# Softmax sums from the exponentials' accumulator, and attention results of two heads in one column group

## What is computed

```
q, k, v  = x @ qkv_weights, split into heads
a        = einsum('aib,ajb->aij', q, k) / 4
a        = tril * a + NEG_INF * (1 - tril)
a        = softmax(a, axis=-1)
heads    = einsum('aij,ajb->aib', a, v)
x        = layernorm(x + heads)
```

## Time and profile before

| | |
|---|---|
| median of 3 runs | 766.68 us (763.91 to 766.88) |
| profiled execution, its time | 762.62 us |
| its span in the profile | 760.7 us |
| mean granted TensorE clock | 0.983 |
| busy over the span: PE, DVE, ACT, POOL | 700.6, 470.8, 449.3, 391.2 us |
| batch stage, first to last exponential | 34.1 to 392.5 us |

### The profile page before, as it was taken

How to read it: one execution, slowest core, us unless ns; L and a number is a source line. 1 busy time by engine, 2 the same in 40 slices (tenths; PEclk the granted TensorE clock), 3 DMA queues, 4 the chain that set the end, 5 groups by cost and what they waited for, 6 DMA issues and landing times.

```text
span 760.7 us, 19153 instructions
## 1 busy us (share of the span) xinstructions
PE 700.6 (92%) x5464; PEld 529.7 (70%) x5465; DVE 470.8 (62%) x1427; ACT 449.3 (59%) x1242; POOL 391.2 (51%) x532
## 2 busy tenths in 40 slices
PE   7968899899999999999997897899999999999983
PEld 6857788788888888888875554555565556565452
DVE  2555578788888889888866554344444444443373
ACT  0268688788888888888863221344444444454154
POOL 1001134235445545544545471477777777777481
PEclk9999999999999999999999999999999999999988
DMA  8744474523223323323455246555555455554883
GB/s 296 260 153 157 134 226 149 191 65 92 72 86 90 81 81 101 110 73 108 113 158 169 80 175 199 146 86 84 84 84 84 84 84 84 84 85 69 250 289 138
DMA packets 84779, 97.98 MB, mean 129 GB/s; under 512 B 12160, under 2 KB 76288, under 8 KB 83680
## 3 DMA queue, kind: packets, MB, share of 16 engines
q1 hardware_dynamic: 59728, 64.03, 27.3%
q0 software_dynamic: 14752, 23.53, 15.6%
q10 hardware_dynamic: 10224, 9.49, 4.7%
HBM read 55.90 MB, written 41.10 MB: 128 GB/s over the span
## 4 chain that ended last, share of the span: by engine, by line
PE 69%; issue 7%; DMA 6%; DVE 6%; POOL 4%; SPq 4%; ACT 2%; ACTq 0%; POOLq 0%; DVEq 0%
PE ps L1034 12%; PE ps L1043 6%; PE ps L797 5%; PE ps L894 4%; PE ps L785 4%; PE ps L762 4%; PE ps L807 4%; PE ps L837 4%; PE ps L897 3%; PE ps L918 3%; PE ps L765 3%; PE ps L817 3%; POOL total L666 3%; DMA attn_only<-in_ctx 2%; PE ps L1020 2%
## 5 line engine op out<-in xcount | busy, mean ns | idle before, releaser
L1109 ACT ACTIVATE prob<-ps,nmax 128x128 f32<-128x128 f32 x512 | 146.9, 379 | 29.8 <-DVE nmax L1308 28.8
L1034 PE MATMUL ps<-first_use,xgT 128*128 x284 | 133.8, 593 | 1.5 <-ACT xgT L1227 1.5
L666 POOL DMA_INDIRECT total<-rot,result_row x71 | 112.1, 1579 | 13.8 <-issue 12.6
L1569 DVE TENSOR_TENSOR tile_parts<-ps,attn_only 128x512 f32<-128x512 f32 x71 | 49.1, 692 | 90.0 <-PE ps L1034 90.0
L1308 DVE TENSOR_REDUCE nmax<-ps 128x4 f32<-128x512 f32 x128 | 82.2, 685 | 21.3 <-PE ps L785 20.2
L599 POOL TENSOR_TENSOR rot<-products 128x128 f32<-128x128 f32 x128 | 61.2, 499 | 65.7 <-DVE products L1318 65.6
L1116 ACT COPY pT<-ps 128x512 f32<-128x512 f32 x128 | 76.9, 601 | 19.2 <-PE ps L797 13.7
L797 PE MATMUL ps<-tf,prob 128*128 128x128 f32 x512 | 78.8, 277 | 6.2 <-ACT pT L1116 6.2
L623 POOL DMA_INDIRECT sent<-packets,pos x64 | 63.4, 991 | 36.9 <-PE ps L785 22.6
L1034 PEld LDWEIGHTS ps<-first_use,xgT 128*128 128x128 f32 x284 | 53.5, 190 | 40.1 <-issue 36.5
L650 POOL TENSOR_TENSOR tile_parts<-tile_parts 128x256 f32<-128x256 f32 x71 | 51.2, 721 | 58.2 <-ACT tile_parts L1222 58.2
(11 more groups left out here) (140 smaller groups left out, 1449.1 us busy)
## 6 DMA issues: line engine op xcount, KB each, us to landing
xg<-sent ACTq DMA_DIRECT2D x68, 130.5 KB, 2.1
first_use<-total SPq DMA_DIRECT2D x12, 512.0 KB, 8.5
total<-zeros POOLq DMA_DIRECT2D x1, 4224.0 KB, 17.8
k_dram<-first_use SPq DMA_DIRECT2D x4, 1024.0 KB, 4.5
attn_only<-in_x_turned SPq DMA_DIRECT2D x32, 128.0 KB, 3.0
attn_only<-k_dram SPq DMA_DIRECT2D x256, 16.0 KB
attn_only<-in_x SPq DMA_DIRECT2D x32, 128.0 KB, 2.7
attn_only<-in_ctx SPq DMA_DIRECT2D x32, 128.0 KB, 2.7
```

The costliest lines, as they stand in the source:

```text
L666: eng.indirect_dma_start(totals[slot % 2], bass.IndirectOffsetOnAxis(ap=result_row[:, slot:slot + 1], axis=0), yw[:, slot % 4, :], None, c ...
L1034: mm = eng.matmul(ps[:, r, :], xgT[:, r, c, :], rw1_sb[:, bass.ds(e * (DC * 2 * FFN) + c * 2 * FFN, 2 * FFN)], start=(c == 0), stop=(c == ...
L1109: ins = eng.activation(prob[:, t % 2, 4 * u + n, :], SCORE[u][:, n * P:(n + 1) * P], ACT.Exp, bias=nmax[:, t % 2, 4 * u + n:4 * u + n + 1])
L1569: eng.tensor_tensor(hid[:, r, :], ps[:, r, :], rb_h[:, bass.ds(e * (2 * FFN), 2 * FFN)], ALU.add).then_inc(hid_set, 1)
```

## The change

Four edits that belong together:

1. Each exponential also gives its row sum to a new tile `den`, by the instruction's accumulating output. `HEAD_OF` says which head stands at which place of which bank.
2. V no longer carries a column of ones. Each head's 32 columns hold 16 of V and 16 zeros: even heads in the first half, odd heads in the second. Two heads write the same 32 rows (one starts the accumulation, the other ends it), so that the 16 heads fill 8 groups of 32 rows, 256 columns of bank 5.
3. The copy to `oT` takes 256 columns in place of 512, and two transposes take the place of four.
4. The reciprocals read `den` and are taken one step earlier, for sequence `n-1`; the multiplication waits for the transposes itself.

```diff
+HEAD_OF = [[2 * u + n % 2 + 8 * (n // 2) for n in range(4)] for u in range(4)]
...
-        HEADS_T = ps[:, 5, :].rearrange("p (x t) -> p x t", t=P)
-        HEADS = ps[:, 5, :].rearrange("p (h v) -> p h v", v=VW)
+        HEADS_T = ps[:, 5, 0:D].rearrange("p (x t) -> p x t", t=P)
+        HEADS = ps[:, 5, 0:D].rearrange("p (h d) -> p h d", d=DH)
...
-        oT = sb("oT", [P, H // CG, P])
+        oT = sb("oT", [P, D // P, P])
+        den = sb("den", [P, 2, H])
...
-            eng.memset(va[:, :, :, DH:DH + 1], 1.0)
...
-                for h in range(H):
-                    lo = h % CG * VW
-                    mm = eng.matmul(HEADS_T[lo:lo + VW, h // CG, :], va[:, t % 3, h, :],
-                                    pT[:, h % 8 // 2, 2 * (h // 8) + h % 2, :], start=True, stop=True)
+                for x in range(D // P):
+                    for e in range(2):
+                        for g in range(CG):
+                            h = 2 * CG * x + 2 * g + e
+                            mm = eng.matmul(HEADS_T[g * VW:(g + 1) * VW, x, :], va[:, t % 3, h, :],
+                                            pT[:, h % 8 // 2, 2 * (h // 8) + h % 2, :], start=(e == 0), stop=(e == 1),
+                                            skip_group_check=True)
...
-                    for b in range(H // CG):
+                    for b in range(D // P):
...
                     ins = eng.activation(prob[:, t % 2, 4 * u + n, :], SCORE[u][:, n * P:(n + 1) * P], ACT.Exp,
-                                         bias=nmax[:, t % 2, 4 * u + n:4 * u + n + 1])
+                                         bias=nmax[:, t % 2, 4 * u + n:4 * u + n + 1],
+                                         accum_out=den[:, t % 2, HEAD_OF[u][n]:HEAD_OF[u][n] + 1])
...
-                    eng.copy(oT[:, :, :].rearrange("p x t -> p (x t)"), ps[:, 5, :]).then_inc(oT_set, 1)
+                    eng.copy(oT[:, :, :].rearrange("p x t -> p (x t)"), ps[:, 5, 0:D]).then_inc(oT_set, 1)
...
-                    eng.copy(va[:, t % 3, :, 0:DH], QV[:, D:2 * D].rearrange("p (h d) -> p h d", d=DH)).then_inc(v_set, 1)
+                    eng.copy(va[:, t % 3, :, :].rearrange("p (j e) (f d) -> p j (e f) d", e=2, d=DH)[:, :, 0:4:3, :],
+                             QV[:, D:2 * D].rearrange("p (j e d) -> p j e d", e=2, d=DH)).then_inc(v_set, 1)
...
-                if live(t2):
-                    eng.wait_ge(heads_turned, t2 + 1)
-                    eng.reciprocal(rden[:, r2, :], HEADS[:, :, DH]).then_inc(den_set, 1)
+                if live(n - 1):
+                    eng.wait_ge(expd, 4 * n)
+                    eng.reciprocal(rden[:, (n - 1) % 2, :], den[:, (n - 1) % 2, :]).then_inc(den_set, 1)
...
                 if live(t2):
+                    eng.wait_ge(heads_turned, t2 + 1)
                     eng.wait_ge(den_set, t2 + 1)
```

More of the change, by code:

```diff
@@ L1469, in step @@
                 if live(t2):
+                    eng.wait_ge(heads_turned, t2 + 1)
                     eng.wait_ge(den_set, t2 + 1)
-                    eng.tensor_tensor(att[:, r2, :].rearrange("p (h d) -> p h d", d=DH), HEADS[:, :, 0:DH],
+                    eng.tensor_tensor(att[:, r2, :].rearrange("p (h d) -> p h d", d=DH), HEADS,
                                       rden[:, r2, :].unsqueeze(2).broadcast_to([P, H, DH]), ALU.mult).then_inc(att_set, 1)
```

## The result

The changed kernel takes 783.74 us (median of 6 runs, 781.11 to 786.45) against 767.32 us before: the ratio is 1.0197, with a 95% interval of 1.0157 to 1.0237. It is slower by 2.0%; the medians differ by 16.4 us. The prediction said 805, which is 38 us more than before, with a range of 774 to 845. The direction and the place were right; the size was not: it forecast more than twice the loss.

What follows compares the result with a forecast made beforehand. PE was taken as the bound, with ACT's ring about 1 us shorter. New step 10.1 + 0.1 + 2.3 = 12.5 us against 11.15, times 28 gives 38 us: 762.6 + 38 = 801, 805 against the median, range 774 to 845.

Steps and rivals of the forecast that it cites:

- The ring from the first exponential over ACT's list to the scaled Q, scores and maximum: Batch-stage cycle through ACT, PE and DVE: 10.1 us without slack against a step of 11.15, to become the longest.
- all holes in ACT's list: ACT's idle gaps between first exponential and scaled Q, 1.0 us per step in all, counted as slack.
- the allowance of 0.1: Per step, for ACT waiting on PE's turn of probability group 2; an allowance, not a measured wait.
- The 28 steps: Of 31 intervals between first exponentials, about 3 are held by something else; 28 x 1.35 = 38 us.
- r = 0.145: Start-to-start cost in us of each accumulator read on ACT; 16 reads add 2.3 us per step.
- my lower end 0.055: Lower bound in us on a read's cost, the fixed part of L1192, an ACT instruction with only immediates.
- the read overlaps but is not free, r about 0.09: Rival on the ACT reads: ring 11.6 us per step, 14 us more, time 780; chance 0.24.
- PE's 0.22: Two of four transposes in L904 go: 0.22 us per step, 7 us over 32 steps, if PE stays the bound.
- PE's ring would be 10.7: PE's own step after the change: about 11.15 - 0.22 - 0.20 = 10.7 us.
- That ends PE's 0.20 us hold before L945: The earlier reciprocal lets DVE's K products start sooner, removing PE's 0.20 us wait per step.
- PE is the longer ring by about 1 us, and no more: In the batch stage, work added to ACT between first exponential and L1192 is paid out of that 1 us.
- The copy of oT, the order of the result matmuls, the memset: Copy 0.22 less on ACT but shortens nothing; paired matmuls cost nothing; dropped prologue memset nothing, 0.18 us if uncovered.

Runs made afterwards that it cites:

- E2: Kernel before the change with only the accumulating sums added to its exponentials, written to a tile nobody reads; ratio 1.0209, median 785.2 us.
- E1: Changed kernel with the accumulating output taken off the exponentials, reciprocals reading ones, result unnormalised; ratio 1.0014 to the kernel before, median 766.9 us.
- E3: Changed kernel with sums on only two of the four exponentials of each bank, other heads unnormalised; ratio 1.0069 to the kernel before, median 771.8 us.
- E6: Changed kernel, all sums, with ACT's copy of group 1 ahead of bank 0's exponentials and x1T's copy behind scaled Q; ratio 1.0137 to before, 770.1 us.

## Why the prediction was wrong

**What bounds the kernel.** Right in its main point. The ring from the first exponential over ACT's list to the scaled Q, scores and maximum became the chain that ends last. It was incomplete: I took all holes in ACT's list for PE's doing, which would vanish when ACT gets later. The hole before the copy of group 2 is a round trip between ACT and PE and stayed whole (0.32 idle in both traces, 0.43 in start-to-start time before and 0.46 after); the allowance of 0.1 for this very wait was too small. And a hole of 0.19 before xv, in the trace of before, I had not seen; 263.63 was possible:

```profile
263.82 0.37 ACT L1159 COPY xv<-ps 128x256 f32<-128x256 f32 x1
```

The two errors, with the 0.1 allowed, nearly cancel, which is luck: 10.1 + 0.1 + 16 x 0.09 = 11.64, against 11.70 measured for that step. The 28 steps are a little many: 28 x 0.58 is 16.2 us, and the batch stage grew by 14.3. The 25 steps outside the start and the arrivals grew by 14.5 and the other six shrank by 0.2.

**The step that failed: r = 0.145.** "I take the exponential's own fixed part" was wrong. The read costs 0.09 start to start, between my lower end 0.055 and the value taken. 16 x 0.055 us too much per step is 0.88 us, and over 28 steps 25 us, which is the distance from 805 to 780; measured were 783.7. This is a term mis-sized and not a mechanism missed, and the rival "the read overlaps but is not free, r about 0.09" named both its price and its time (780), at 0.24. The reads' durations, 0.19 to 0.27, lie near gexp's 0.24, but only the distance of the starts counts. From the Trainium skill's page "ScalarE: Activation LUTs", section "What ACT_TABLE_LOAD costs", I had estimated 94 ns for a one-element instruction with immediates; the trace's 0.09 for the read agrees with that estimate, though the page gives no price for the read itself. The argument that the read "has to deliver a per-partition value" and so costs like a per-partition operand had nothing behind it: what makes the exponential's fixed part longer than that of L1192 may be its operand coming in, and the read has none. That reason I have not tested.

**PE's 0.22.** Right that it is worth nothing beside the late ACT (E2). Wrong that PE's ring would be 10.7 without it: E1 shows 11.22, and 11.02 in its early steps. "That ends PE's 0.20 us hold before L945" failed. The K products do start 0.15 earlier in E1 (1.67 after the first exponential against 1.82), but scx stands behind the Q products, and those wait for PE; the hold is 0.26. "PE is the longer ring by about 1 us, and no more" was too simple as well: in E3 eight reads, 0.73 in all, cost 0.13 to 0.19 per step.

**The copy of oT, the order of the result matmuls, the memset.** Costed at nothing. E1, with all of them in, is 0.11 us per step under before in the early steps and 0.04 over it in the later ones, and its result matmuls hold the chain for 1.01 us as before. So none of them shows a cost, if they do not offset each other.

**The stages behind.** Forecast as untouched. The profiled pair seems to say otherwise; the medians leave some 2 us for them, and the last section deals with the rest.

**What would show it.** 512 reads as a group: yes. Four exponentials in 1.7 us: no, 1.51 from 270.64 to the end of the fourth read. No idle time before x1T: yes. PE idle 1.8 us per step: no, 0.56 in the step from 270.64. Steps of 12.5: no, 11.76. ACT's L1197 as what the scores wait for: yes, as the chain shows.

## What to carry to other kernels

An output that "comes for free" with an instruction can be a second instruction behind it; cost it by start-to-start distances of short neighbours, with both ends, and put the number where it lies between the likeliest rows before choosing by an argument. When an engine is 97% busy, that does not mean that work taken from it shortens the step: look at the events in mid-step that come at a fixed delay from another engine, and ask on which side of them the saved work stands. And a wait between two engines that hand one buffer back and forth is part of the ring and does not vanish when one of them gets slower. Before steps of two profiles are compared at the level of a tenth of a microsecond, look whether the same wait ends at the same delay in both; here a late signal, and not the edit, made up to 0.2 us of such differences.

## What the runs showed of the hardware

**A read of the accumulator** takes 0.19 to 0.27 us and costs 0.09 start to start behind a 128-column exponential. Durations grow along an unbroken run of such pairs, with the starts at even distances: the reads go from 0.19 (270.91) on, the exponentials from 0.36, and the last read of the step reads

```profile
278.99 0.27 ACT L1113 ACTIVATION_READ_ACCUMULATOR prob<-ps,nmax 128x1 f32 x1
```

The scaled Q behind them takes 0.47 where it took 0.39, and after an idle stretch the durations are short again. So in such a run the ends fall behind the starts, by 0.08 us at the end of a step.

**The granted clock scatters in the stretch behind the batches, with the sums and without.** From the last first group of exponentials to the end it is 375.1 us before and 383.3 after (span less start), but 378.6 in E1, 375.4 in E3, 370.5 in E6 and 382.6 in E2, with mean clocks over the span of 0.983, 0.974, 0.980, 0.977, 0.987 and 0.968. E6 has all the sums and the shortest stretch. The kernel before by itself took 754.30 us at a mean clock of 0.988 and 764.88 at 0.978 on one chip. In windows of the changed kernel the loss can be seen (PE, PEld, DVE, ACT, POOL busy, clock, DMA share, GB/s):

```profile
410.00:420.00 10.00, 8.56 (x72) 7.52 (x72) 5.52 (x19) 3.73 (x8) 5.31 (x9) 0.84 0.87 286
420.00:430.00 10.00, 9.23 (x58) 6.13 (x49) 3.86 (x11) 1.87 (x4) 4.35 (x7) 0.91 0.37 130
430.00:440.00 10.00, 7.80 (x32) 6.70 (x33) 5.35 (x22) 1.98 (x5) 4.88 (x8) 0.66 0.16 55
```

A mean of 0.66 in a window is a mixture of the 2.4 and the 1.2 GHz level. The same 32 result matmuls took 1.01 us in the chain in the batch stage and 1.86 here:

```profile
419.04 1.86 PE ps L810 x32
```

PE had waited 1.27 us shortly before them, ahead of L997. The kernel before has such windows too (0.83 from 415 to 425 us). This puts 8 us of scatter and more into any single pair of profiles of this kernel, half of what the change moved, so the starts within the batch stage were the better measure.
